# Linear attention on Trainium2: another order of the summary steps, and the two low parts exchanged between VectorE and GpSimd

## The reference, cut to what matters

```
q, gate = query @ Wq.T, sigmoid(query @ Wg.T + bg)
k, v = split(kv @ Wkv.T)                     # kv is the context of the batch
feature_map(x) = where(x > 0, x + 1, exp(x)) # on q and on k
kv_summary = einsum('bhsd,bhse->bhde', k, v) # sum over the 1500 rows
k_sum = k.sum(axis=-2)
attn = einsum('bhld,bhde->bhle', q, kv_summary) / (q . k_sum + 1e-6)
out = attn * gate @ Wo.T
```

## Time and profile before

| what | value |
|---|---|
| median of 3 runs | 3339.28 us (3338.1 to 3340.88) |
| profiled execution, its own time | 3340.39 us |
| its span from first to last instruction | 3338.4 us |
| TensorE busy | 3125.9 us, 94% |
| VectorE busy | 2222.3 us, 67% |
| ScalarE busy | 1815.7 us, 54% |
| GpSimd busy | 1770.9 us, 53% |
| mean granted TensorE clock | 0.972 |

### The profile page before, as it was taken

The page is one execution under the profiler, slowest core; times in us unless marked ns, Lnnn a source line. Parts: engine busy times, 40 slices in busy tenths (PEclk is TensorE's granted clock), DMA queues, the critical chain, the costliest instruction groups (busy, mean ns, idle before and its releaser), DMA issues. The chain is left out here.

```text
span 3338.4 us, 65287 instructions
## 1 busy us (share of the span) xinstructions
PE 3125.9 (94%) x23304; PEld 2824.4 (85%) x23304; DVE 2222.3 (67%) x3434; ACT 1815.7 (54%) x3277; POOL 1770.9 (53%) x1890
## 2 busy tenths in 40 slices
PE   5999999996999999579999999999999999995999
PEld 4999999995999999558888888888888888884998
DVE  5888888884222222537877777787777777775554
ACT  3666666661323323146666666666666666662443
POOL 3877777771433433145565656555655565541332
PEclk9999999996999999789999999999999999996999
DMA  5544445421100100011111111011111111104000
GB/s 143 151 140 137 146 147 147 145 76 38 37 22 19 38 19 0 0 61 36 54 54 31 50 54 52 28 54 54 45 35 54 54 45 36 54 12 151 6 6 11
DMA packets 88460, 203.85 MB, mean 61 GB/s; under 512 B 25408, under 2 KB 64688, under 8 KB 83376
## 3 DMA queue, kind: packets, MB, share of 16 engines
q1 hardware_dynamic: 86288, 202.93, 19.4%
q10 hardware_dynamic: 2112, 0.12, 0.1%
HBM read 184.94 MB, written 14.42 MB: 60 GB/s over the span
## 5 line engine op out<-in xcount | busy, mean ns | idle before, releaser
L1437 DVE TENSOR_TENSOR a_probT<-a_p,a_probT 125x448 fp32r<-125x448 f32 x768 | 459.2, 617 | 155.1 <-ACT a_probT L1370 152.0
L1370 ACT CAST a_probT<-a_p 125x448 fp32r<-125x448 f32 x768 | 395.7, 537 | 255.8 <-PE a_p L1554 254.6
L1431 DVE TENSOR_REDUCE a_mxs<-a_s 112x1 f32<-112x1500 f32 x256 | 439.8, 1718 | 96.6 <-PE a_s L1542 93.0
L1569 PE MATMUL a_o<-a_probT,a_val 125*64 125x224 f32 x3072 | 473.3, 278 | 1.7 <-DVE a_probT L1437 0.9
L1554 PE MATMUL a_p<-ident,a_prob 112*125 112x112 f32 x3072 | 438.6, 274 | 2.5 <-DVE a_probT L1437 2.3
L1554 PEld LDWEIGHTS a_p<-ident,a_prob 112*125 112x125 f32 x3072 | 387.9, 188 | 43.7 <-issue 26.7
L1363 ACT ACTIVATE a_prob<-a_s,a_mxs 112x1500 f32<-112x1500 f32 x256 | 389.4, 1521 | 15.6 <-DVE a_mxs L1431 14.5
L1569 PEld LDWEIGHTS a_o<-a_probT,a_val 125*64 125x64 f32 x3072 | 338.0, 136 | 37.9 <-issue 24.5
L725 POOL TENSOR_TENSOR e_hT_lo<-e_h,e_hT_hi 128x448 fp32r<-128x448 f32 x144 | 167.7, 1165 | 353.3 <-ACT e_hT_hi L772 353.3
L438 POOL TENSOR_TENSOR l_rows_lo<-l_raw,l_rows_hi 125x512 fp32r<-125x512 f32 x192 | 267.1, 1391 | 163.6 <-ACT l_rows_hi L477 163.6
L1287 POOL TENSOR_TENSOR a_two<-a_picked 64x224 f32<-64x224 f32 x128 | 84.1, 657 | 434.3 <-DVE a_picked L1449 434.3
(11 more groups left out here) (279 smaller groups left out, 9266.1 us busy)
## 6 DMA issues: line engine op xcount, KB each, us to landing
l_rawT<-in_ctxT SPq DMA_DIRECT2D x32, 1500.0 KB, 6.2
a_rawT<-in_ctxT SPq DMA_DIRECT2D x32, 1500.0 KB, 6.2
l_raw<-in_ctx SPq DMA_DIRECT2D x32, 1344.0 KB
e_gu_in<-in_L_ffn_w_gate_up SPq DMA_DIRECT2D x8, 1024.0 KB, 4.9
W_hi<-w_out_hi SPq DMA_DIRECT2D x32, 192.0 KB, 2.4
W_lo<-w_out_lo SPq DMA_DIRECT2D x32, 192.0 KB, 2.4
l_raw<-in_ctx SPq DMA_DIRECT2D x32, 156.0 KB
e_down_in<-in_L_ffn_w_down SPq DMA_DIRECT2D x8, 512.0 KB, 5.8
```

Source lines behind the costliest of these rows:

```text
L1370: act.copy(p_target(j, f, 0), p_source(i)).then_inc(p_hi[i], 1)
L1431: dve.tensor_reduce(mxs[:, j:j + 1], s_bank[0:TT, :, 0:GW], AX.XY, ALU.max, negate=True).then_inc(max_done, 1)
L1437: dve.tensor_tensor(p_target(j, f, 1), p_source(i), p_target(j, f, 0).bitcast(F32), ALU.subtract).then_inc(p_read[i], 1)
L1569: mm = pe.matmul(o_bank[0:2 * PW, at:at + 2 * TT], flat(val[:, ch, j, :, :]), flat(probT[j % 2][:, ch, :, :]), start=(ch == 0), stop=(ch = ...
```

## The change

In each slot ScalarE now takes the exponential of k straight from the PSUM bank, and VectorE takes min(expk, 1) afterwards, from SBUF to SBUF, in place of min(k, 0) from PSUM before it. VectorE makes `phik.lo` in place of `ctxT.lo`, and GpSimd makes `ctxT.lo` in place of `phik.lo`. The summary steps move: `g_copy` stands in slot 2 of the next batch (behind the features), `gt` in slot 4, ScalarE's copy of `GT` and the scaled queries in slot 4 still but behind the copy of `rows.hi`, `kv` in slot 5, and `kv_copy`, `numden` with the first half of the division (`nd_invert`), and the rest (`nd_use`) in slots 0, 1 and 3 of the batch after the next. The diff, without what only moves along:

```diff
@@ gpsimd
+            def t_low(b, u, g):
+                pool.wait_ge(t_hi, NP * b + g + 1)
+                cols = slice(g * CP * CH, (g + 1) * CP * CH)
+                pool.tensor_tensor(ctxT.lo[:, :, cols], rawT[u][:, :, cols],
+                                   ctxT.hi[:, :, cols].bitcast(F32), ALU.subtract).then_inc(t_lo, 1)
...
                 for g in range(NP):
+                    if g + 2 < NP:
+                        t_low(b, u, g + 2)
+                    elif not last:
+                        t_low(b + 1, 1 - u, g + 2 - NP)
                     sl = slice(g * CP, (g + 1) * CP)
                     pool.wait_ge(rows_hi, NP * b + g + 1)
                     pool.tensor_tensor(rows.lo[:, sl, 0:D], raw[u][:, sl, :], rows.hi[:, sl, 0:D].bitcast(F32),
                                        ALU.subtract).then_inc(rows_lo, 1)
-                    pool.wait_ge(phi_hi, NP * b + g + 1)
-                    pool.tensor_tensor(flat(phik.lo[:, sl, :]), phif[:, g % 2, :], flat(phik.hi[:, sl, :]).bitcast(F32),
-                                       ALU.subtract).then_inc(phi_lo, 1)
@@ scalar
+                    act.wait_ge(k_full, NP * b + g + 1)
+                    if g >= 2 or not first:
+                        act.wait_ge(phi_done, NP * b + g - 1)
+                    act.activation(expk[:, g % 2, :], k_bank[g % 2][0:CH, :], ACT.Exp).then_inc(exp_done, 1)
...
                     if g == 4 and not first:
                         act.wait_ge(gt_full, b)
                         act.copy(flat(GT[:, :, :]), gt_bank[:, :]).then_inc(gt_read, 1)
                         scale_queries(b - 1)
-                    act.wait_ge(min_done, NP * b + g + 1)
-                    act.activation(expk[:, g % 2, :], expk[:, g % 2, :], ACT.Exp).then_inc(exp_done, 1)
@@ vector
-            def batch(b, u, first=False, last=False):
+            def batch(b, u, first=False, known=False, last=False):
                 for g in range(NP):
...
                     dve.wait_ge(exp_done, NP * b + g + 1)
+                    dve.tensor_scalar(expk[:, g % 2, :], expk[:, g % 2, :], 1.0, None, ALU.min).then_inc(min_done, 1)
+                    dve.wait_ge(min_done, NP * b + g + 1)
                     if g >= 2 or not first:
                         dve.wait_ge(phi_lo, NP * b + g - 1)
                     dve.scalar_tensor_tensor(out=phif[:, g % 2, :], in0=k_bank[g % 2][0:CH, :], scalar=0.0,
                                              in1=expk[:, g % 2, :], op0=ALU.max, op1=ALU.add).then_inc(phi_done, 1)
-                if not first:
-                    nd_use(b - 1)
+                    if g == 0 and not first and not known:
+                        kv_copy(b - 2)
+                    if g == 1 and not first and not known:
+                        nd_invert(b - 2)
+                    if g == 2 and not first:
+                        g_copy(b - 1, 1 - u)
+                    if g == 3 and not first and not known:
+                        nd_use(b - 2)
+                    dve.wait_ge(phi_hi, NP * b + g + 1)
+                    dve.tensor_tensor(flat(phik.lo[:, g * CP:(g + 1) * CP, :]), phif[:, g % 2, :],
+                                      flat(phik.hi[:, g * CP:(g + 1) * CP, :]).bitcast(F32), ALU.subtract).then_inc(phi_lo, 1)
@@ tensor
-                    if g == 5 and not first:
-                        numden(b - 1)
...
-                    if g == 3 and not first:
+                    if g == 1 and not first and not known:
+                        numden(b - 2)
+                    if g == 4 and not first:
                         gt(b - 1)
-                    if g == 4 and not first:
+                    if g == 5 and not first:
                         kv(b - 1, not known)
```

More of the change, by code:

```diff
@@ L432, in _, with batch @@
             pool.memset(rows.lo[:, :, D:CW].bitcast(F32), 0.0).then_inc(ones_set, 1)
-            def batch(b, u):
+            def t_low(b, u, g):
[3 more added lines that the diff above has]
+                                   ctxT.hi[:, :, cols].bitcast(F32), ALU.subtract).then_inc(t_lo, 1)
+            def batch(b, u, last=False):
                 for g in range(NP):
+                    if g + 2 < NP:
+                        t_low(b, u, g + 2)
+                    elif not last:
+                        t_low(b + 1, 1 - u, g + 2 - NP)
                     sl = slice(g * CP, (g + 1) * CP)
@@ L439, in batch @@
                                        ALU.subtract).then_inc(rows_lo, 1)
-                    pool.wait_ge(phi_hi, NP * b + g + 1)
-                    pool.tensor_tensor(flat(phik.lo[:, sl, :]), phif[:, g % 2, :], flat(phik.hi[:, sl, :]).bitcast(F32),
-                                       ALU.subtract).then_inc(phi_lo, 1)
-            with pool.Fori(0, B // 2) as i:
+            t_low(0, 0, 0)
+            t_low(0, 0, 1)
+            with pool.Fori(0, B // 2 - 1) as i:
                 batch(2 * i, 0)
                 batch(2 * i + 1, 1)
+            batch(B - 2, 0)
+            batch(B - 1, 1, last=True)
         @block.scalar
@@ L465, in batch @@
                         t_copy(1 - u, n + u, g + 2 - NP)
-                    if g == 4 and not first:
-                        act.wait_ge(gt_full, b)
-                        act.copy(flat(GT[:, :, :]), gt_bank[:, :]).then_inc(gt_read, 1)
-                        scale_queries(b - 1)
-                    act.wait_ge(min_done, NP * b + g + 1)
-                    act.activation(expk[:, g % 2, :], expk[:, g % 2, :], ACT.Exp).then_inc(exp_done, 1)
+                    act.wait_ge(k_full, NP * b + g + 1)
+                    if g >= 2 or not first:
+                        act.wait_ge(phi_done, NP * b + g - 1)
+                    act.activation(expk[:, g % 2, :], k_bank[g % 2][0:CH, :], ACT.Exp).then_inc(exp_done, 1)
                     if g == 0:
@@ L477, in batch @@
                     act.copy(rows.hi[:, g * CP:(g + 1) * CP, 0:D], raw[u][:, g * CP:(g + 1) * CP, :]).then_inc(rows_hi, 1)
+                    if g == 4 and not first:
+                        act.wait_ge(gt_full, b)
+                        act.copy(flat(GT[:, :, :]), gt_bank[:, :]).then_inc(gt_read, 1)
+                        scale_queries(b - 1)
                     act.wait_ge(phi_done, NP * b + g + 1)
@@ L511, in kv_copy, with nd_invert @@
                                   K["blockmask"][:, :].unsqueeze(1).to_broadcast([P, KC, P]), ALU.mult).then_inc(kv_read, 1)
-            def nd_use(b):
+            def nd_invert(b):
                 dve.wait_ge(nd_full, b + 1)
@@ L517, in nd_use @@
                 dve.reciprocal(den[:, :, :], den[:, :, :]).then_inc(den_inv, 1)
+            def nd_use(b):
                 dve.wait_ge(den_inv, b + 1)
@@ L522, in nd_use @@
                 dve.tensor_tensor(K["attT"][:, :, bass.ds(b * L, L)], nd[:, :, 0, :], den[:, :, :], ALU.mult).then_inc(nd_read, 1)
[L524 to L528, removed]
-            def batch(b, u, first=False, last=False):
-                for g in range(NP):
-                    if g == 3 and not first:
-                        g_copy(b - 1, 1 - u)
-                    if g == 5 and not first:
[L535 to L543, removed]
+            def batch(b, u, first=False, known=False, last=False):
+                for g in range(NP):
                     dve.wait_ge(exp_done, NP * b + g + 1)
+                    dve.tensor_scalar(expk[:, g % 2, :], expk[:, g % 2, :], 1.0, None, ALU.min).then_inc(min_done, 1)
+                    dve.wait_ge(min_done, NP * b + g + 1)
                     if g >= 2 or not first:
@@ L549, in batch @@
                                              in1=expk[:, g % 2, :], op0=ALU.max, op1=ALU.add).then_inc(phi_done, 1)
-                if not first:
-                    nd_use(b - 1)
-            t_low(0, 0, 0)
-            t_low(0, 0, 1)
+                    if g == 0 and not first and not known:
[9 more added lines that the diff above has]
+                                      flat(phik.hi[:, g * CP:(g + 1) * CP, :]).bitcast(F32), ALU.subtract).then_inc(phi_lo, 1)
             batch(0, 0, first=True)
-            with dve.Fori(0, B // 2 - 1) as i:
+            batch(1, 1, known=True)
+            with dve.Fori(1, B // 2 - 1) as i:
+                batch(2 * i, 0)
                 batch(2 * i + 1, 1)
-                batch(2 * i + 2, 0)
+            batch(B - 2, 0)
             batch(B - 1, 1, last=True)
+            kv_copy(B - 2)
+            nd_invert(B - 2)
             g_copy(B - 1, 1)
+            nd_use(B - 2)
             kv_copy(B - 1)
+            nd_invert(B - 1)
             nd_use(B - 1)
@@ L640, in _ @@
                 g_group(B - 1, 1, g, False)
+            numden(B - 2)
             gt(B - 1)
```

## The result

| | before | after |
|---|---|---|
| median | 3339.18 us (14 runs) | 3348.86 us (14 runs) |
| range of the runs | 3335.32 to 3340.88 | 3344.95 to 3351.48 |
| span of the profiled execution | 3338.4 us | 3347.4 us |

The account below looks back on a forecast made before the run. The prediction saw the stage bound by a loop through VectorE, ScalarE and GpSimd, TensorE close behind. Slots of 3.52 us plus 0.38 a batch gave +8.2, the end +1: +9.2 on 3339.28, forecast 3348.5 us, range 3335 to 3365.

Parts of the forecast that it names:

- The bound of before: Old stage: a loop through VectorE, ScalarE and GpSimd sets 21.43 us a batch, TensorE close behind at 20.02 busy.
- The sum: Whole kernel: last high-feature copy 8.2 us later, at 754.2, plus an estimated 1 at the end: +9.2, giving 3348.5 us.
- The minimum waits for the port: VectorE's SBUF-to-SBUF minimum, 0.42 us alone, waits behind GpSimd's `ctxT.lo` until 2.35, ends at 2.77, shows about 1.05.
- The slot of 3.52: Period between ScalarE's high-feature copies: 1.22 + 1.13 + 0.42 + 0.04 + 0.71 = 3.52 us.
- The summary steps: Moved steps in their new slots: `nd_invert` +0.30 us in slot 1, `nd_use` +0.08 in slot 3, the others nothing.
- the gate product: Product of `nd_use` in slot 3: some 0.28 us alone, waits for the port until 0.26; slot cost +0.08.
- +0.38 a batch: Summary steps' charge on each batch: 6 x 3.52 + 0.38 = 21.50 us, against 21.43 before.
- the +1: End of the stage: last `phik.lo`, and `numden` and `nd_invert` ahead of the last `g_copy`, estimated at +1 us.
- the hand-over: Rival: the minimum loses the port to `rows.lo`; 3587 us if always, 3468 every second time; chance 0.27, 0.15 for always.
- The fast rival: Rival: the minimum isn't stopped or goes first, TensorE's 19.9 us a batch decide: -46, 3293 us; chance 0.13.
- The costlier summary: Rival: `phik.lo` pushed behind `ctxT.lo` in slots 1 and 3, 1.2 us each: +70, 3418 us; chance 0.06.
- The signs: Changed profile: minimum about 1.05 us, `rows.lo` about 1.4, ScalarE waits about 0.9 a slot, TensorE's idle time not shorter.

Follow-up runs that it names:

- e6: The kernel before with only the summary steps moved to their new places, minimum and low parts as before: 3286.1 us, ratio 0.9841.
- e2: The changed kernel with GpSimd making only half of `ctxT.lo`, the other half left zero: 3280.6 us, ratio 0.9824.
- e10: The changed kernel with the minimum left out, which computes another function: 3278.6 us, ratio 0.9827 to the kernel before.
- e3: The changed kernel with the minimum from PSUM again, ahead of the exponential and a slot early: 3282.4 us, ratio 0.983.
- e9: The changed kernel with a second minimum behind the first, with its own wait: 3621.1 us, ratio 1.085.
- e1: The changed kernel with ScalarE's exponential ahead of the context copy: 3332.2 us, ratio 0.998 to the kernel before.
- e5: The changed kernel with GpSimd on `phik.lo` and VectorE on `ctxT.lo` again: 3369.8 us, ratio 1.0094.

## Why the prediction was right

- **The bound of before** (a loop through VectorE, ScalarE and GpSimd, TensorE close behind) held in part only. The prediction spread 21.43 us evenly over six slots and put VectorE's lateness down to `ctxT.lo` at the port. e6 leaves those meetings at the port as they are (the median of `ctxT.lo` is 1.36 us in both traces) and still reaches 3286 us. What kept before off TensorE's floor was the summary steps in their old places: 53 us of the 58 between before and the fastest version. The sum didn't need this reading, since it built the new slots from the durations of single operations.
- **The minimum waits for the port** held: 1.10 us for 0.42 alone, at 2.78 in the slot. e2 is the proof by intervention (68 us), e10 and e3 give its whole price, 66 to 70 us.
- **The slot of 3.52** held at 3.51. One slot of each batch differs, as the one from 303.22, which took 3.63. In it the features start 0.12 us behind the minimum (306.00 to 306.12) in place of 0.04. I didn't have this, and no run shows its cause.
- **The summary steps**: slot 1 costs 0.24 over 3.51 (310.37 to 314.12 is 3.75), forecast 0.30; the gate product was 0.64 in place of its 0.27, as the port said. That a batch came out at 21.52 for 21.50 is luck in part: the 0.06 too much here stands against the 0.1 that was missing in the slot from 303.22. The forecast charged the later summary with +0.38 a batch and credited the shorter chain to "the slot". It never priced the move by itself. Measured alone it is a gain of 53 us in the old order and 25 in the new. The sum came out right because it was made slot by slot, not part by part, so that no price of a part entered it.
- **The sum**: the last high-feature copy is at 753.00, forecast 754.2. The two last slots without `ctxT.lo` gave 2.2 us back, which the sum had overlooked, and the end of the stage took 1.0 us more than the +1 (the span grew by 9.0, the last copy came 7.0 later). These two errors cancel in part, which is luck.
- **The rivals**: the hand-over was never lost. The longest of 192 minima is 1.46, where a lost one would show 2.3. The fast rival's condition was wrong, since the minimum is stopped; its price was right in kind (TensorE decides) and 12 us too high. I gave it 19.9 us a batch; in e2 and e10, where TensorE has no gap, a batch takes 19.4. The costlier summary did not occur: `phik.lo` is over 0.70 us once, in the first slots, and never pushed behind `ctxT.lo` in slots 1 and 3.
- **The signs**: two of those named did not come. ScalarE waits 1.3 us a slot for the features, not 0.9; the prediction's own slot gives 1.34, from 2.18 to 3.52. And TensorE's idle time did get shorter, 21 of 360 us from 300 to 660 us for 24 before. Neither enters the sum.
- Where the Trainium skill stood beside it (SBUF — State Buffer, Who interferes with whom): the second to ask fully blocks; e9 agrees on either side of one hand-over, with 1.10 and 1.38 us for a minimum of 0.42. The same section says that the one that starts first keeps the pair for the whole instruction. By the rows the pair comes free a little before the recorded end: the minimum ends at 306.00, so its 0.42 us began at 305.58, while `ctxT.lo` is shown to 305.71.

So the answer to where the change's effect went: a gain of 53 us (summary), taken back and more by the new minimum, which costs 84 us without the exchange of the low parts and 66 with it. The exchange in its turn is worth some 20 us beside the new minimum.

## What to carry to other kernels

Price an operation not by its duration but by the port it takes: the form of the minimum that is faster alone (0.42 for 0.69 us) was slower by 66 us in this loop, since it had to wait for GpSimd's `ctxT.lo`. When a large edit has several parts, make each alone; here the best part (the later summary, 3286 us in e6_sum_alone) was hidden by the worst, and without the worst (e3_min_psum, 3282 us) the rest beats both kernels. And follow a shared resource through more than one slot, with both sides' next requests, as e1, e5 and e9 show: a wait that is removed in one place lets another operation come early and collide there.

## What the runs showed of the hardware that was not expected

The hand-over of the port was regular in this loop: behind `ctxT.lo` the minimum always went ahead of the `rows.lo` that followed (189 of 189, all under 1.5 us), though the experts stage had shown one case of the other kind, 4.896 us. That case isn't chance either: it stands in all twelve traces, with 4.894 to 4.897 us. What makes it different stays open; no run took it up. Between two minima 0.04 us apart GpSimd gets in nearly each time (e9: 191 of 192, median 1.385 us). And the exponential from PSUM takes 0.59 us, from SBUF 0.63.
